# Folding the masked layers' weights for all batches ahead of the loop, and a new order of the loop's phases

## The reference, cut to what matters

```python
# layers 0 and 2 (grouped)
q = (rmsnorm(x, norm_w) @ wq).reshape(B, T, 16, 32)
k, v = cond @ wk, cond @ wv                     # 4 heads of 32
attn = softmax(einsum('btgrd,bsgd->bgrts', q, k) / sqrt(32))
x = x + einsum('bgrts,bsgd->btgrd', attn, v) @ wo
# layers 1 and 3 (masked)
q, k, v = x @ Wq, cond @ Wk, cond @ Wv          # 16 heads of 64
probs = softmax(einsum('bhqd,bhkd->bhqk', q, k) / 8 + col_bias)
x = x + einsum('bhqk,bhkd->bhqd', probs, v) @ Wo + bo
```

## Time and profile before

| | |
|---|---|
| median of 3 runs | 1689.45 us (1689.1 to 1689.66) |
| the profiled execution's own time | 1690.16 us |
| its span, first to last instruction | 1688.0 us |
| mean granted TensorE clock | 0.998 |
| PE / DVE / POOL / ACT busy | 96% / 62% / 46% / 41% of the span |
| DMA | 138.64 MB, 82 GB/s over the span |

### The profile page before, as it was taken

How to read it: one execution, slowest core, us unless ns; L and a number is a source line. 1 busy time by engine, 2 the same in 40 slices (tenths; PEclk the granted TensorE clock), 3 DMA queues, 4 the chain that set the end, 5 groups by cost and what they waited for, 6 DMA issues and landing times.

```text
span 1688.0 us, 25162 instructions
## 1 busy us (share of the span) xinstructions
PE 1617.7 (96%) x8416; PEld 1339.1 (79%) x8416; DVE 1038.8 (62%) x1758; ACT 684.9 (41%) x1193; POOL 782.1 (46%) x745
## 2 busy tenths in 40 slices
PE   8989999999999999999999999999999999999997
PEld 8988778877787878878788777878788787887786
DVE  5545666467655675567654776557664676557763
ACT  3445433453335532453334623354324533345321
POOL 2747334572356542573356623574345723565310
PEclk9999999999999999999999999999999999999999
DMA  7942221222222310322212312322212222222001
GB/s 276 321 137 79 82 63 38 82 77 75 63 93 71 107 39 24 108 82 82 63 52 78 111 31 63 108 81 82 63 38 80 72 82 63 81 77 88 25 1 50
DMA packets 91906, 138.64 MB, mean 82 GB/s; under 512 B 50560, under 2 KB 55168, under 8 KB 85504
## 3 DMA queue, kind: packets, MB, share of 16 engines
q1 hardware_dynamic: 89312, 119.60, 22.6%
q10 hardware_dynamic: 2304, 16.78, 2.4%
q0 software_dynamic: 160, 0.53, 0.1%
HBM read 114.33 MB, written 22.55 MB: 81 GB/s over the span
## 4 chain that ended last, share of the span: by engine, by line
PE 82%; DVE 8%; ACT 4%; issue 3%; POOL 2%; DMA 1%; DVEq 0%; ACTq 0%; POOLq 0%; SPq 0%
PE OB L351 11%; PE OB L353 11%; PE OB L352 11%; PE SB L351 10%; PE SB L353 9%; PE SB L352 9%; PE TB L480 4%; PE MX L351 3%; PE MX L353 2%; PE MX L352 2%; DVE pT L771 2%; PE MX L480 1%; DVE x L863 1%; DVE foldM L771 1%; POOL xqhl L1021 1%
## 5 line engine op out<-in xcount | busy, mean ns | idle before, releaser
L1013 POOL TENSOR_TENSOR prob<-prob,small 128x512 f32<-128x512 f32 x256 | 266.9, 1044 | 586.1 <-DVE small L853 586.1
L727 ACT ACTIVATE prob<-prob 128x512 f32<-128x512 f32 x128 | 81.0, 632 | 507.3 <-DVE prob L841 507.3
L1007 POOL TENSOR_TENSOR prob<-prob,small 128x512 f32<-128x512 f32 x128 | 133.6, 1044 | 168.9 <-DVE small L829 168.1
L351 PE MATMUL OB<-pT,foldN 128*128 128x512 f32 x512 | 205.7, 402 | 6.3 <-DVE pT L771 6.3
L351 PE MATMUL SB<-foldM,xhl 128*128 128x512 f32 x512 | 201.2, 393 | 0.3
L353 PE MATMUL OB<-pT,foldN 128*128 128x512 f32 x512 | 200.4, 391 | 0.0
L352 PE MATMUL OB<-pT,foldN 128*128 128x512 f32 x512 | 200.2, 391 | 0.0
L353 PE MATMUL SB<-foldM,xhl 128*128 128x512 f32 x512 | 199.7, 390 | 0.0
L352 PE MATMUL SB<-foldM,xhl 128*128 128x512 f32 x512 | 199.2, 389 | 0.0
L829 DVE TENSOR_REDUCE small<-prob 128x8 f32<-128x512 f32 x128 | 87.7, 685 | 143.3 <-ACT prob L697 143.2
L835 DVE SCALAR_TENSOR_TENSOR prob<-SB,aux 128x512 f32<-128x512 f32 x128 | 88.2, 689 | 142.1 <-PE SB L353 142.1
(11 more groups left out here) (139 smaller groups left out, 3853.6 us busy)
## 6 DMA issues: line engine op xcount, KB each, us to landing
prob<-in_wkvM_dram SPq DMA_DIRECT2D x32, 512.0 KB, 5.9
ring<-in_wqM_dram SPq DMA_DIRECT2D x64, 256.0 KB, 2.8
ring<-in_woM_dram SPq DMA_DIRECT2D x64, 256.0 KB, 3.4
out_dram<-x ACTq DMA_DIRECT2D x16, 1024.0 KB, 3.9
wraw<-in_wqG_dram SPq DMA_DIRECT2D x8, 1024.0 KB, 7.5
ring<-in_xT_dram SPq DMA_DIRECT2D x32, 256.0 KB, 4.3
wraw<-in_woG_dram SPq DMA_DIRECT2D x8, 1024.0 KB, 5.1
x<-in_xT_dram SPq DMA_DIRECT2D x8, 1024.0 KB, 5.1
```

Of the source, the lines that this page charges most:

```text
L351: pe.matmul(out, a_hi, b_hi, start=start, stop=False)
L727: act.activation(own, own, ACT.Exp).then_inc(S["exped"], 1)
L1007: pool.tensor_tensor(own, own, hmax[u % 2].unsqueeze(2).broadcast_to([P, HH, KEYS]), ALU.subtract).then_inc(S["evac"], 1)
L1013: pool.tensor_tensor(own, own, rsum[u % 2].unsqueeze(2).broadcast_to([P, HH, KEYS]), ALU.mult).then_inc(S["normed"], 1)
```

## The change

1. **The fold moves to the prologue.** Behind each `m_made(n)` the prologue now runs `folding(n - 1)`: 4 x `three` = 12 fp32r matmuls of 512 columns, for all four batches at once, into the banks FB = OB[2], OB[3], TB, MX. So `m_made` has two banks, OB[0] and OB[1], instead of four. Keys or values are taken straight from the bank into a block-diagonal high/low pair `bd` in SBUF (`kv_hi`, `kv_lo`), and not stored. The weights of the step are loaded (`f_load`, 256 KB) and split (`f_hi`, `f_lo`). The four results are copied to staging tiles (`taken_out`, two on ACT, two on DVE) and stored to DRAM by SP (`f_store`, four DMAs of 256 KB): sFM for foldM, each DMA as 512 pieces of 512 bytes, the four batches' parts 2 MiB apart; sFN for foldN, in rows of 2048 bytes. Steps 0 to 7 and 16 to 23 write sFM, the others sFN.
2. **The loop loads the folded weights** through ring: 16 loads of 256 KB an iteration, as many as before, in ph 1 to 3. ACT makes the high parts (`part_hi`), DVE the low parts of the first 4 and POOL those of the other 12, one beside each step. `fold_bound`, `kv_load` and the tile kv are gone.
3. **Order and banks.** The query sums go to the output banks OB instead of TB, MX, SB; the sums of squares go to SB1. The first transposes of a phase run inside `q_bound` or ahead of the last `out_part`s. In ph 2 and ph 3 the masked scores of step u run one step later than before. The low part of the new x is split between POOL (chunks 0, 2) and DVE (1, 3).
4. The last store is cut into four, each behind its own `xnew`.

```diff
-        PB = [TB, MX, SB[0], SB[1]]
+        FB = [OB[2], OB[3], TB, MX]
...
+            def f_load(n):
+                if n >= 4:
+                    sp.wait_ge(S["f_lo"], n - 3)
+                src = (wqM if n // KC % 2 == 0 else woM)[n // (2 * KC), n % KC]
+                sp.dma_start(f32[n % 4], src).then_inc(f_in[n % 4], 16)
+
+            def f_store(n):
+                lp, t = n // (2 * KC), n % KC
+                for o in range(4):
+                    if o < 2:
+                        sp.wait_ge(S["ev_a"], 2 * n + o + 1)
+                    else:
+                        sp.wait_ge(S["ev_d"], 2 * n + o - 1)
+                    if n // KC % 2 == 0:
+                        sp.dma_start(sFM[lp, :, t // 4, o, :, (t % 4) * P:(t % 4 + 1) * P].rearrange("b p n -> p b n"),
+                                     staged(n, o).rearrange("p (b n) -> p b n", b=BATCH)).then_inc(f_st[n % 2], 16)
+                    else:
+                        sp.dma_start(sFN[lp, o, t], staged(n, o)).then_inc(f_st[n % 2], 16)
...
+            def folding(n):
+                if n == 0:
+                    pe.wait_ge(S["zero"], 3)
+                pe.wait_ge(S["taken"], m_step(n) + 1)
+                pe.wait_ge(S["f_lo"], n + 1)
+                w, kv = fhl[n % 2], bd[n % 2]
+                for o in range(4):
+                    cut = slice(o * P, (o + 1) * P)
+                    if n > 0 and o < 2:
+                        pe.wait_ge(S["ev_a"], 2 * n + o - 1)
+                    elif n > 0:
+                        pe.wait_ge(S["ev_d"], 2 * n + o - 3)
+                    if n // KC % 2 == 0:
+                        last = three(FB[o][:, :], w[:, 0, cut], w[:, 1, cut], kv[:, 0, :], kv[:, 1, :], True, True)
+                    else:
+                        last = three(FB[o][:, :], kv[:, 0, cut], kv[:, 1, cut], w[:, 0, :], w[:, 1, :], True, True)
+                    last.then_inc(S["folded"], 1)
...
                 for c in range(DC):
+                    if c == DC - 1 and not (first and ph == 0):
+                        transposes(it, ph, 0, first)
+                        if ph == 0:
+                            transposes(it, ph, 1, first)
...
+            def masked_grouped(it, first):
+
+                for s in range(1, STEPS):
+                    transposes(it, 2, s, first)
+                    product(it, 2, s - 1, first)
+                    if s >= 3:
+                        out_part(it, 2, (s - 3) // 2, (s - 3) % 2)
+                    scores(it, 2, s - 1, first)
+                product(it, 2, KC - 1, first)
+                out_part(it, 2, 2, 1)
+                scores(it, 2, STEPS - 1, first)
+                transposes(it, 3, 0, first)
+                out_part(it, 2, 3, 0)
+                out_part(it, 2, 3, 1)
+
+            def masked_masked(it, first):
+
+                transposes(it, 3, 1, first)
+                for s in range(1, STEPS):
+                    if s % 2 == 0:
+                        transposes(it, 3, s, first)
+                        transposes(it, 3, s + 1, first)
+                    product(it, 3, s - 1, first)
+                    scores(it, 3, s - 1, first)
+                product(it, 3, KC - 1, first)
+                scores(it, 3, STEPS - 1, first)
...
+            def part_hi(it, i):
+                act.wait_ge(ld_ring[i % 4], 16 * (6 * it + 2 + i // 4 + 1))
+                act.activation(fold_part(i, 0), ring[:, i % 4, :], ACT.Copy).then_inc(S["fold_hi"], 1)
...
+            def part_lo(it, i):
+                pool.wait_ge(S["fold_hi"], 16 * it + i + 1)
+                pool.tensor_tensor(fold_part(i, 1), ring[:, i % 4, :], fold_part(i, 0).bitcast(F32), ALU.subtract
+                                   ).then_inc(S["fb_lo"], 1)
```

More of the change, by code:

```diff
@@ L307, in body @@
                     sp.dma_start(X[0][:, :, :], x_of(0)).then_inc(S["ld_x0"], 16)
[L308 to L315 removed]
+                for c in range(DC):
+                    ring_load(8 + c, sFM[lp, b, 0, c])
                 if first:
@@ new lines, in grouped_grouped @@
+            def grouped_grouped(it, first):
+                for u in range(STEPS):
+                    if u > 0:
+                        transposes(it, 1, u, first)
+                        product(it, 1, u - 1, first)
+                    if u >= 3:
+                        out_part(it, 1, (u - 3) // 2, (u - 3) % 2)
+                    scores(it, 1, u, first)
+                product(it, 1, KC - 1, first)
+                out_part(it, 1, 2, 1)
+                transposes(it, 2, 0, first)
+                out_part(it, 1, 3, 0)
+                out_part(it, 1, 3, 1)
@@ L911, in _ @@
                 pt_lo(ITS, 0, t)
-            for c in range(DC):
-                xnew(ITS, 0, c)
+            xnew(ITS, 0)
         @block.gpsimd
```

802 lines of the change are left out of this document (459 added, 343 removed).

## The result

The changed kernel takes 1669.14 us (median of four runs, 1666.99 to 1671.88), beside 1689.28 us (1688.04 to 1689.66) for the kernel before on the same chip: a ratio of 0.9883, interval 0.987 to 0.9895. It is faster by 1.2%, where 2.7% was forecast. The profiled execution took 1669.71 us; against the forecast's sum on the profiled time, 1643.9 us, 25.8 us are missing.

A forecast was written before the change was run, and what follows sets the result against it. PE, busy 96% of the span, was taken as the bound. 1690.2 - 143.2 + 87.2 + 3 + 6 - 2.3 + 8 - 5 = 1643.9, less 0.7 for the median: 1643 us; range 1616 to 1674.

The forecast's parts named there:

- Fold out of the loop: In all eight iterations both fold stretches on PE go, 17.9 us an iteration: -143.2 us.
- fold into the prologue: In the prologue, 32 steps of 12 matmuls of 512 columns on PE, with nothing beside them: +87.2 us.
- Rival E: Copies and subtractions moved into the loop's steps hold PE as long there, 5.8 us an iteration: 1689 us, chance 0.04.
- Query sums in OB: At the loop's queries, sums wait only for xnew, 0.68 behind each finished output bank, so no hole: no cost.
- Splitting the loaded weights: In ph 1 to 3, 12 low parts on POOL and 4 on DVE fit in idle time: costed at nothing.
- Early transposes: At the start of ph 1, 0.7 of PE's 1.6 us idle is taken back each iteration: -5 us.
- Masked scores a step later: At the starts of ph 2 and ph 3, holes of 0.3 and 0.7 us, 1.0 an iteration: +8 us.
- The transfers: In the prologue, demand and supply of DMA bandwidth meet; uneven arrivals cost +6 us.
- Rival C: Transfers pace the prologue at 279 GB/s, a step takes 6.6 us, 24 us instead of 6: 1661 us, chance 0.18.
- Rival D: Prologue stores of 512-byte pieces crawl at 131 GB/s, 69 us instead of 6: slower, 1706 us, chance 0.08.
- B: Later scores hide the xb chain, ph 1 loses its 1.6 us, transfers keep up: 1622 us, chance 0.14.
- The entry into the loop: Ahead of the loop, PE's wait for POOL's low part of x falls from 3.68 to about 1.4 us: -2.3.

The follow-up runs named there:

- e16: Changed kernel with e2, e4, e6, e7 and both edits of e15 together: 1638.7 us, ratio 0.9699 to the kernel before.
- e15: Changed kernel with the woG load behind the four loads of x, and the third chunk of x ahead of ph 3's last exponential and normalisations: 1659.5 us.
- e2: Changed kernel with POOL's low parts of the loaded weights made one place earlier against the normalisations in ph 2: 1658.7 us.
- e11: Changed kernel with PE's masked scores back in their own step and POOL's low parts of the loaded weights one place earlier: 1685.5 us.
- e7: Changed kernel with all four low parts of the new x on DVE instead of two on DVE and two on POOL: 1665.2 us.
- e6: Changed kernel with the 1 MB load of wqG issued behind four more weight loads in the prologue: 1663.5 us.
- e4: Changed kernel with sFM stored in rows of 2048 bytes and the loop's load gathering pieces of 512 bytes: 1662.7 us.
- e8: Changed kernel with e2, e4, e6 and POOL's low parts of x's first two chunks ahead of a normalisation: 1652.1 us.
- e12: Changed kernel with e2, e4, e6, e7 and ph 3's last product moved behind the last masked scores: 1648.7 us.
- e3: Changed kernel with only PE's masked scores moved back into their own step in ph 2 and ph 3: 1730.4 us.

## Why the forecast was right in direction and wrong in size

- *Fold out of the loop*, -17.9 us an iteration, and *fold into the prologue*, +87.2: both right. The steps in the undisturbed stretch are 5.6 us apart and the matmul count is met, and with its new holes closed (e16) an iteration is 17.2 us shorter than before. Rival E (the copies hold PE) is out with it.
- *The eight steps beside the first grouped scores*, +3: this was not needed. They are 6.34 us apart, the 6.3 of PE's own work. That iteration 0 took just the 199.6 us of the terms is luck: these 3 us too many stood against some 3 us of the new holes named next, which iteration 0 has as well (e16 takes 196.9).
- *Query sums in OB, "so no hole"*, and with it the entry into the body at nothing: **this step failed**. PE waits 1.77 us there instead of 0.2. My step looked at the banks and not at what now comes together at this edge: the last probabilities of ph 3 a step later ahead of the low part of x on ACT and POOL, and the load of woG, now issued 1.34 us ahead of PE's branch. 1.2 us an iteration by e15, 8 to 9 us in all.
- *Splitting the loaded weights*, costed at nothing because "eight more of 1.28 fit" in POOL's busy time: **this step failed as well**. The time was there and the order was not, since each low part stands behind a normalisation that waits for DVE. 1.3 us an iteration by e2, 10 us in all. A busy share told nothing about when an operation is done.
- *POOL's busy time* rose by 100 us, not 82: low parts of 1.29 to 1.34 us, those of the new x at 1.52, and 256 normalisations that take 1.10 us instead of 1.04. The wait for pT at the start of ph 3 is there, as said.
- *Early transposes*, -0.7 an iteration: **this step failed too**, there is no gain in the holes of ph 1. Forecast 5 us, measured none (0.4 us an iteration the other way). PE waits there for DVE's low parts of pT; no run undid this edit alone, so why it gave nothing stays open.
- *Masked scores a step later*: the mechanism was right, the sizes were off both ways. Without it an iteration is 2.8 us longer (e11), where I had some 1.2 at the first boundary. The holes left are 0.99 at the start of ph 2 (0.3 forecast) and 0.60 at that of ph 3 (0.7). DVE's low parts were priced at 0.68 and take 1.37 beside POOL's (e7: 0.5 us an iteration).
- *The transfers*, +6: the term was too small. Its bounds held it, but with the entry the delay is about 13 us: the burst at the start (5.4 us in this trace, 3.3 to 4 of them by e6), which I had not costed, and waits for stores, most of them of 512-byte pieces (some 5 to 6 us by e4, the lower clock behind them included). Rival C was the nearer for the prologue, though not by its mechanism: the steps are not 6.6 us apart throughout. They are 5.6 but for the fourth, which starts 11.0 us behind the third, the other first ones, which hold more matmuls (7.4 to 9.0) and the three that waited for stores. Rival D (stores at 131 GB/s) is out, and so is B: the holes did not close, new ones opened.
- *The entry into the loop*, -2.3: wrong. PE's hole there is 3.25 us, not 1.4, and was 3.68 before. The sum took ACT's copies to be ready while PE still works; they wait 3.48 us for a store of sFM to leave the staging tile, and x's parts stand behind them. Even with long rows the hole is 2.3 to 3.7 us (e4, e8, e12, e16).

The three failed steps of the loop add up to 1.2 + 1.3 + 0.7 = 3.2 us, against 3.0 missing in an iteration; that it fits so well is in part chance, since the larger hole at the start of ph 2 and the 0.4 us lost in ph 1 aren't in it. The prologue gives the other 7. The forecast expected too much of an order that was changed in many places at once, and put several of the edits at nothing (the query sums in OB, the split of the loaded weights) without asking what stands ahead of each operation.

## What to carry to other kernels

Where a change re-orders several engines' programs, ask at every phase boundary what each queue has in front of the operation that the bound engine needs; free time in a stretch doesn't hide an operation that stands behind a wait. A hole that doesn't move when its named releaser is made earlier may have a second cover of nearly the same length: take both away before ruling either out. And look at what transfers run beside a loop's edge, and at the row length that a store writes when the DMA engines are full.

## What the runs showed of the hardware

- PE's branch at a loop's edge takes 3.3 to 3.9 us, and 4.9 to 5.7 us (all but one 5.1 or more) where a 1 MB load is issued 1.34 us ahead of it (share 1.00). A load issued 3.3 us ahead of it or 1.15 us behind its start did not lengthen it. It ends 1.3 to 1.5 us after a 16 KB packet of instructions, which starts some 1 us after it, or 2.5 to 3.4 us where the load is in its way. PE's queue of 3.7 us of matmuls covers the short branch and not the long one. At its last, untaken pass it takes 0.08 us.
- A wait of 3.4 us on PE was followed by 6 us at a granted clock of 0.50 (e3), in every iteration.
- Stores in 512-byte pieces against rows of 2048 bytes, in the prologue's mix and with the engines full: 318 against 366 GB/s (308 to 336 in 13 profiles, 362 to 378 in four). A pitch of 2 or 2.25 MiB made no difference that could be told.
- A subtraction on DVE with both inputs in SBUF took 1369 ns beside the like on POOL and 687 alone; POOL's went from 1276 to 1524 ns.
